# Token records of 32 bytes in place of token rows, gathered rows, and weight splits ahead of the attention loop

## The reference, cut to what is computed

```python
# attention
xn = layernorm(x);  Q, K, V = xn @ Wq.T + bq, ...          # per head
scores = Q K^T / 4 + lam * (tanh(Q) J) tanh(K)^T           # causal
x = x + (softmax(scores) V) @ Wo.T + bo
# feed-forward: xf is the layernorm of x
xf = layernorm(x)
xn = layernorm(xf) * ln_scale + ln_bias
probs = softmax(xn @ gate_w.T);  top 2, divided by their sum + 1e-5  -> w
out = swiglu(xf, sWg, sWu, sWd)                            # shared expert
for e in range(8):
    out = out + w[:, e] * swiglu(xf, Wg[e], Wu[e], Wd[e])
return x + out
```

## Time and profile before

| | before |
|---|---|
| time, median of 3 runs (lowest, highest) | 2176.34 us (2170.82, 2176.91) |
| the profiled execution: its time, its span | 2184.37 us, 2182.7 us |
| mean granted TensorE clock in it | 0.965 of full speed |
| PE, DVE, ACT, POOL busy | 1983.4, 1246.0, 1080.8, 799.5 us |
| moved by DMA | 246.08 MB in 156640 packets |

### The profile page before, as it was taken

The page is one execution under the profiler, slowest core; times in us unless marked ns, Lnnn a source line. Parts: engine busy times, 40 slices in busy tenths (PEclk is TensorE's granted clock), DMA queues, the critical chain, the costliest instruction groups (busy, mean ns, idle before and its releaser), DMA issues. The chain is left out here.

```text
span 2182.7 us, 48214 instructions
## 1 busy us (share of the span) xinstructions
PE 1983.4 (91%) x14698; PEld 1300.2 (60%) x14767; DVE 1246.0 (57%) x3875; ACT 1080.8 (50%) x2352; POOL 799.5 (37%) x1164
## 2 busy tenths in 40 slices
PE   2789999999999999999986999997999999999997
PEld 1344444554444444444444887875777777777776
DVE  5556677666677666676653964442454544545454
ACT  1155555555555555555542454451555555555553
POOL 3023333333233333233332046661444444444443
PEclk8589999999999999999987999998999999999999
DMA  7124443434433444434313345553873333333332
GB/s 238 42 84 117 133 127 113 127 112 120 138 114 120 115 118 138 126 115 129 107 62 105 116 160 206 196 177 101 216 201 55 58 53 57 56 54 59 53 55 35
DMA packets 156640, 246.08 MB, mean 113 GB/s; under 512 B 29408, under 2 KB 90592, under 8 KB 156480
## 3 DMA queue, kind: packets, MB, share of 16 engines
q1 hardware_dynamic: 120960, 189.24, 28.2%
q0 software_dynamic: 32064, 53.44, 11.9%
q10 hardware_dynamic: 3456, 1.34, 0.2%
HBM read 111.89 MB, written 90.50 MB: 93 GB/s over the span
## 5 line engine op out<-in xcount | busy, mean ns | idle before, releaser
L646 DVE CUSTOM_DVE_ANT_0 ps_rows<-ps_rows,maskrow 128x512 f32<-128x512 f32 (+3 forms) x1024 | 484.1, 514 | 309.6 <-PE ps_rows L501 308.8
L589 ACT ACTIVATE probs<-ps_cols 128x512 f32<-128x512 f32 (+3 forms) x1024 | 392.1, 435 | 394.1 <-PE ps_cols L512 387.5
L501 PE MATMUL ps_rows<-ks,qs 32*128 32x512 f32 (+3 forms) x2048 | 429.7, 494 | 85.3 <-DVE mx L646 47.4
L508 PE MATMUL ps_cols<-qs,ks 32*128 32x512 f32 (+3 forms) x2048 | 421.9, 488 | 2.5 <-ACT probs L589 2.4
L1590 POOL DMA_INDIRECT out_dram<-y_e,to x135 | 215.5, 1596 | 348.9 <-DMA out_dram<-y_e,to 227.6
L765 POOL TENSOR_TENSOR pace<-eps 1x1 f32<-1x1 f32 x256 | 57.9, 226 | 766.4 <-ACT probs L589 766.4
L501 PEld LDWEIGHTS ps_rows<-ks,qs 32*128 32x128 f32 x2048 | 162.2, 188 | 295.7 <-DVE mx L646 246.7
L512 PE MATMUL ps_cols<-mT,ones_r 32*128 32x512 f32 (+3 forms) x1024 | 287.3, 554 | 0.0
L1719 DVE TENSOR_TENSOR h_lo<-ps_h,h_hi 128x512 fp32r<-128x512 f32 x135 | 93.4, 692 | 231.5 <-ACT h_hi L1694 231.5
L1688 ACT ACTIVATE sg_e<-ps_ge 128x512 f32<-128x512 f32 x135 | 80.7, 598 | 261.2 <-PE ps_ge L1612 255.5
L525 PE MATMUL ps_o<-probs,vt 128*32 128x512 f32 (+3 forms) x2048 | 193.7, 450 | 0.8 <-POOL probs L767 0.8
(11 more groups left out here) (211 smaller groups left out, 3799.9 us busy)
## 6 DMA issues: line engine op xcount, KB each, us to landing
xs_d<-zrows SPq DMA_DIRECT2D x45, 408.0 KB, 2.9
xr<-xs_d POOLq DMA_DIRECT2D x135, 136.0 KB, 3.2
whi_d<-w_sh SPq DMA_DIRECT2D x16, 768.0 KB, 3.8
w_hi<-whi_d SPq DMA_DIRECT2D x24, 512.0 KB
xn<-in_L_attn_x_dram SPq DMA_DIRECT2D x16, 512.0 KB, 5.3
ks<-k_lin SPq DMA_DIRECT2D x64, 128.0 KB, 2.9
ks<-k_tan SPq DMA_DIRECT2D x64, 128.0 KB, 3.7
qs<-q_lin SPq DMA_DIRECT2D x64, 128.0 KB, 2.4
```

The costliest lines, as they stand in the source:

```text
L501: mm = nc.tensor.matmul(ps_rows[bank_of(row_no(g, it, h))][:, 0:(it + 1) * P], qs[at:at + STRIP, d.par, g, it * P:(it + 1) * P], ks[at:at ...
L508: nc.tensor.matmul(ps_cols[bank_of(col_no(n, s, e))][:, jt * P:S], ks[at:at + STRIP, b.par, gc, jt * P:(jt + 1) * P], qs[at:at + STRIP, b. ...
L589: nc.scalar.activation(probs[:, n % 2, 2 * (1 - s) + e, jt * P:S], ps_cols[bank_of(col_no(n, s, e))][:, jt * P:S], ACT.Exp).then_inc(exp_d ...
L646: nc.vector.tensor_tensor_reduce(out=bank, in0=bank, in1=maskrow[:, (TT - 1 - it) * P:S], scale=1.0, scalar=LOWEST, op0=ALU.add, op1=ALU.m ...
```

## The change

1. The splits of wk, wq, wv move on POOL from the head of the attention loop into the setup block, behind `bq_q` and ahead of `gws`; TensorE no longer waits for them by name, since all engines meet at the block's end.
2. `xs_d` is gone. In its place is `meta_d`, a record of 8 floats (32 bytes) for each slot row: destination, share, source row, and the scale and shift of the layernorm. Zeroing it takes 5 DMAs in batch 0 instead of 45 over 15 batches.
3. In the front stage ScalarE makes no rows, and `xw` isn't loaded. POOL scatters records (`place[:, t, r]`), 128 indirect DMAs as before, waits for all, loads the whole of `meta_d` into the chip, makes two index tables out of it and gathers the rows of the first two slots. VectorE writes two more columns of `place` and works out the record's address, as records lie partition by partition (five operations in place of one, for each of two choices).
4. In the expert stage POOL gathers a slot's rows by index out of the residual `x1_d`, three slots ahead; VectorE normalises them into `xh` with two columns of `meta`, two slots ahead, and copies the source rows (`frm`) and destinations (`to`) of later slots; TensorE transposes `xh`. `share` is read where it lies, in `meta`.

```diff
             pool.wait_ge(s_w, 16 * 16)
             nc.gpsimd.tensor_scalar(bq_q[:], bq_c[:], 0.25, None, ALU.mult)
+            for at, (parts, whole) in enumerate(((wkp, wk), (wqp, wq), (wvp, wv))):
+                nc.gpsimd.tensor_copy(parts[:, 0], whole[:]).then_inc(s_parts, 1)
+                pool.wait_ge(s_parts, at * 2 + 1)
+                nc.gpsimd.tensor_tensor(parts[:, 1], whole[:], parts[:, 0].bitcast(F32), ALU.subtract).then_inc(s_parts, 1)
...
-                if n in (9, 10, 11) and b.at_least(0) and b.at_most(NB - 2):
-
-                    at = b.v * ZR + n - 9
-                    dest = xs_z[at] if b.fixed else xs_z[bass.ds(at, 1)].rearrange("o p n -> (o p) n")
-                    sp.dma_start(dest, zrows[:]).then_inc(xs_zeroed, 16)
+                if b.off == 0 and 9 <= n < 9 + ZR:
+
+                    sp.dma_start(meta_z[n - 9], zrows[:]).then_inc(xs_zeroed, 16)
...
-                nc.scalar.activation(row[q][:, :, 0:D], xw[:, bt % AHEAD, t % TT].unsqueeze(1).to_broadcast([P, 2, D]), ACT.Identity,
-                                     bias=nmr[:, t:t + 1], scale=rstd2[:, t:t + 1]).then_inc(normed, 1)
-                nc.scalar.activation(row[q][:, :, D:D + 2], place[:, t], ACT.Copy).then_inc(normed, 1)
...
         pool.wait_ge(pos_ready, 2)
+        pool.wait_ge(placed, 2)
         for t in range(NT):
-            q = t % RING
-            pool.wait_ge(normed, (t + 1) * 2)
             for r in range(2):
-                nc.gpsimd.indirect_dma_start(xs_d[:, :], bass.IndirectOffsetOnAxis(ap=pos[:, t, r:r + 1], axis=0),
-                                             row[q][:, r], None).then_inc(scattered[q], 16)
-        for q in range(RING):
-            pool.wait_ge(scattered[q], (NT - q + RING - 1) // RING * 32)
+                nc.gpsimd.indirect_dma_start(meta_d[:, :], bass.IndirectOffsetOnAxis(ap=pos[:, t, r:r + 1], axis=0),
+                                             place[:, t, r], None).then_inc(scattered, 16)
+        pool.wait_ge(scattered, NT * 2 * 16)
+        pool.dma_start(meta[:].rearrange("p s w -> p (s w)"), meta_d.rearrange("(p s) w -> p (s w)", p=P)).then_inc(meta_in, 16)
+        pool.wait_ge(meta_in, 16)
...
+        nc.vector.tensor_copy(place[:, :, :, SCALE], rstd2[:].unsqueeze(2).to_broadcast([P, NT, 2])).then_inc(placed, 1)
+        nc.vector.tensor_copy(place[:, :, :, SHIFT], nmr[:].unsqueeze(2).to_broadcast([P, NT, 2])).then_inc(placed, 1)
         beside()
         dve.wait_ge(ranked, 1)
...
         def step(s):
-            if exists(s) and s.at_most(NSLOT - 3):
...
-                pool.dma_start(xr[:, s.par], rows_of(xs_v, s.plus(2))).then_inc(x_loaded[s.par], 16)
+            gather(s.plus(3))
...
+        def norm(s):
+
+            if exists(s):
+                dve.wait_ge(x_loaded[s.par], (s.half() + 1) * 16)
+                if s.at_least(2):
+                    dve.wait_ge(tx_ready, s.v - 1)
+                nc.vector.tensor_scalar(xh[:, s.par], xr[:, s.par], column(meta, s, SCALE), column(meta, s, SHIFT), ALU.mult, ALU.add)\
+                    .then_inc(xn_ready, 1)
```

## The result

The changed kernel takes 2314.18 us in the median (2310.98 to 2319.10, 4 runs) against 2176.62 for the kernel before: a ratio of 1.064, 95% interval [1.0612, 1.0667]. It is 137.6 us slower, where the prediction had it 20 us faster. Its profiled execution took 2319.1 us, span 2317.2, clock 0.939.

A forecast was written before the change was run, and what follows sets the result against it. What counts was taken to be what TensorE waits for in each stage. The terms, 4.2 + 0 + 0.5 - 27.3 - 1.3 + 0 = -24 us, gave 2160 us on the profiled execution and 2156 us for the median, range 2145 to 2186.

The forecast's parts named there:

- the front stage's: Front stage: TensorE's late rounds beside the row scatters go with the row traffic, -27.3 us, bounds 0 and -27.3.
- The rival that was at hand: Front stage: the stalls come from POOL's indirect DMAs as such, not their bytes, and stay; 2180 us, chance 0.18.
- Setup: Setup block: the splits moved there make the attention loop start +4.2 us later, bounds +3 and +5.75.
- Zeroing: Attention loop: 40 fewer zeroing DMAs on SP's queue change nothing, 0 us, bounds 0 and -17.
- The rank round: Front stage: VectorE's two copies into `place` ahead of the wait for ranks, +0.5 us (0 to +1.2).
- POOL's chain: Front stage: record scatters 1.27 us apart to about 1424, then load, small operations and gathers, done by 1440, hidden.
- The rival of late scatters: Front stage: scatters of 32-byte packets take 2.0 us, end at 1517 and cut the gain; 2170 us, chance 0.05.
- Start of the experts: Expert stage's start: the first gate product waits only for the first weight pair, -1.3 us, bounds 0 and -1.7.
- The loop: Expert loop: VectorE's normalisation and POOL's gather are hidden, 0 us.
- the rival by which scatter-adds become the bound: Expert loop, POOL: normalisation delays each scatter-add by 0.407 us, +47 us; 2203 us, chance 0.13 (scatter-adds or VectorE).
- The two readings of the median: Profiled execution's extra 8.0 us is spread evenly (2152 us) or part of the stalls (2160 us); the middle was taken.

The follow-up runs named there:

- the middle gap: A POOL memset of 128x300 behind each scatter, about 1.48 us apart: 2159.43 us (0.9934) on the kernel before, 2168.69 us on the changed kernel.

## Why the prediction was wrong

**The step that failed** is the front stage's: "I take all, **-27.3**, as row traffic is the only part that changes with the loss", with bounds of 0 and -27.3. Where it had -27.3, the front grew by 124.6 us. Row traffic was not all that changed: the rhythm of the scatters did too, and the loss goes with it. Before, POOL waited for rows again and again, 128 scatters in 216 us, and each burst cost little; records wait for nothing, and one burst of 128 costs 151 us. The stalls' size was read rightly: the front before lost 300.0 - 273.2 = 26.8 us in the profile, and goes to 273.11 with the middle gap alone. Their cause was not, and so 0, meant as the worst case of the term, was no bound at all. The rows that misled were the earlier trace rows: 12 scatters in a window without loss were taken as proof that issue alone doesn't stall. They showed that twelve in a burst don't, in that window. The rival that was at hand ("They come from POOL's indirect DMAs as such") was priced as if the rhythm stayed (2180); the prediction itself had worked out that 128 scatters would follow each other without a wait.

**Setup.** +4.2 was sized well at its place: `jb` ends at 23.23 against 19.28, +3.95, and the first k product starts at 37.11 against 34.22, +2.9; with the splits back it is at 34.22 again. What is left of it at the front stage isn't settled: the first down products lie between 1216.3 and 1222.2 in nine profiles with the splits in the setup, and between 1209.1 and 1219.3 in eight without.

**Zeroing.** Right at 0: a batch takes 66.37 us with and without it. **The rank round**: 21.26 us against 20.98, +0.3 for +0.5. **POOL's chain**: right, 1.27 us apart and 10 us of load, tables and gathers; its end, 1442.9, would have been hidden without the stall too, since the front without loss would end near 1221.5 + 273.4 = 1494.9. The rival of late scatters was priced wrongly at 2170: scatters done at 1517 and 10 us of chain behind them end at 1527, 34 us behind the stage's end as forecast (1515.8 + 4.2 + 0.5 - 27.3 = 1493.2), which makes about 2190. It did not occur.

**Start of the experts.** The first gate product stands 4.46 us behind the first weights' issue (1650.57 and 1646.11) and 6.33 before: -1.9 for -1.3. It was not kept: the first up product waits for the second weight pair and comes 0.6 us earlier, and the fifth sigmoid stands 27.4 us behind that issue, where it was 26.3 before. In between, TensorE's clock differs. Having waited for both weight pairs (3.26 and 0.95 us), it is at the lower level until 1659.1, 13.0 us behind the issue, and before only until 1525.9, 10.1 us behind it. Windows 10 to 13 us behind the issue, with the change and before:

```profile
1656.10:1659.10 3.00, 3.00 (x10) 1.67 (x7) 1.08 (x3) 0.00 (x0) 0.00 (x0) 0.50 0.64 243
```

```profile
1525.80:1528.80 3.00, 3.00 (x17) 1.99 (x16) 1.24 (x4) 0.89 (x3) 0.22 (x1) 0.98 0.84 261
```

**The loop.** TensorE paces it as forecast, and the rival by which scatter-adds become the bound did not occur: POOL's scatter-adds take 1588 ns, and it still idles ahead of them. A slot is 4.813 us against 4.786, 3.2 us over 122 slots, for which I had 0; neither normalisation nor gather is shown as its cause. The Trainium skill, DMA: Bandwidth & Descriptors, section SWDGE vs HWDGE vs iDMA, has VectorE in a 2-port mode hold up GpSimd's descriptors; here no scatter-add was lengthened (1588 ns in the mean, 1596 before); whether `xh` runs in that mode no run shows. The same page of the Trainium skill, section Specifications, puts transfers under 512 bytes below line rate; here the 32-byte scatters kept the 0.96 us of rows, and the last had landed 1.45 us after the end of its issue, so no run shows a cost of it.

**The two readings of the median.** "Part of the stalls" was nearer: the middle gap takes 27 us from the front of the kernel before in the profile and 14 from its median.

## What to carry to other kernels

Before taking away what an engine waits for, ask what its queue does without the wait: here the wait for rows was what kept the bursts of POOL's indirect DMAs short, and TensorE running. In this kernel it paid to issue indirect DMAs beside TensorE's work singly and some 1.5 us apart, with an idle operation between them, and not so far apart that the last ones end behind TensorE's work, as at 1.66 us; plain DMAs needed no gap. And a stall that the profile puts down to "remote" or "issue" has no known cause: as the worst case of its term take that it goes on without a pause, and not that it stays as it is.

## What the runs showed that I had not expected

Long trains of POOL's indirect DMAs hold up TensorE when these are 1.29 us apart or less and not at 1.48. The stall came with both widths (32 and 1088 bytes), both numbers of packets (64 and 128) and both directions that were run, and stayed away at 1.48 us with records and with rows; plain DMAs 0.55 us apart don't cause it. In the changed kernel a result of TensorE is then announced 18 us late, and a run of matmuls goes on at one in 2.7 us. What indirect DMAs and TensorE share is not shown by these runs. Each execution timed here was also recorded by the profiler, so whether the recording takes part isn't shown either. POOL's scatter-adds are not lengthened by VectorE, but VectorE's `xh` is by them: 599 ns in the median of the 122 that a scatter-add covers, 408 for the 8 that stand beside no work of POOL, like the operation in the earlier trace rows. All together:

```profile
L1718 DVE TENSOR_SCALAR xh<-xr,meta x135: 406/597/715, 1646.1 to 2293.8; 128x256 f32<-128x256 f32 x135
```
